# Post-norm attention and FP4 feed-forward block, eight batches on one core: a value projection moved across the batch boundary, and the last batch stripped of its look-ahead

## The reference

```python
x = layernorm(x + attention(x, w_qkv))        # 16 heads of 32, softmax over 1024 keys, scale 1/sqrt(512)
xq, hq = fp4(x), fp4(silu(gate) * y)          # blockwise FP4 (blocks of 16), gate and y are xq @ fp4(w_gate).T, xq @ fp4(w_up).T
x = layernorm(x + hq @ fp4(w_down).T)         # inner width 1408
```

## Time and profile before

| | us |
|---|---|
| median of 3 runs | 3785.34 (3785.06 to 3785.47) |
| the profiled execution's own time | 3785.02 |
| its span, first to last instruction | 3783.2 |
| TensorE (PE) busy | 3609.3 (95%) |
| VectorE (DVE) busy | 3116.5 (82%) |
| GpSimd (POOL) busy | 2473.9 (65%) |
| ScalarE (ACT) busy | 1752.2 (46%) |
| mean granted TensorE clock | 0.991 of full |
| chain that ended last | PE 79%, DVE 10%, POOL 2%, DMA 2% |

### The profile page before, as it was taken

One profiled execution on the slowest core, in us unless ns is written; L12 is line 12 of the kernel. 1 busy time (PEld: TensorE's weight loads), 2 busy tenths in 40 slices (PEclk: granted clock), 3 DMA queues, 4 the chain that ended last, 5 costly groups with the idle time before them and its releaser, 6 DMA issues.

```text
span 3783.2 us, 59181 instructions
## 1 busy us (share of the span) xinstructions
PE 3609.3 (95%) x21563; PEld 1602.5 (42%) x21563; DVE 3116.5 (82%) x4894; ACT 1752.2 (46%) x3090; POOL 2473.9 (65%) x1606
## 2 busy tenths in 40 slices
PE   3799999999999999999999999999999999999999
PEld 2344444344444444343444444434444344434344
DVE  9877898778977889777887789878897778977888
ACT  3466424663256622565236642366424663256622
POOL 2288645985469844797448964588545984479844
PEclk8999999999999999999999999999999999999999
DMA  5211232012311133111331122201232112310133
GB/s 180 88 28 35 67 70 63 25 40 68 73 47 35 35 79 70 47 28 34 89 73 32 35 63 66 71 18 44 64 72 55 30 39 72 75 48 27 32 89 71
DMA packets 358962, 215.21 MB, mean 57 GB/s; under 512 B 280592, under 2 KB 307984, under 8 KB 358544
## 3 DMA queue, kind: packets, MB, share of 16 engines
q1 hardware_dynamic: 358672, 211.43, 21.7%
HBM read 76.28 MB, written 19.66 MB: 25 GB/s over the span
## 4 chain that ended last, share of the span: by engine, by line
PE 79%; DVE 10%; issue 2%; DMA 2%; POOL 2%; ACT 1%; SPq 0%; DVEq 0%; ACTq 0%; POOLq 0%
PE SC L1686 18%; PE CT L1650 10%; PE R L709 9%; PE SC L1635 9%; PE R L689 8%; DVE mx L619 6%; PE R L1686 6%; PE R L1708 6%; PE CT L1708 6%; PE R L699 4%; PE R L721 2%; PE R L731 1%; POOL wd L1236 1%; DVE split L613 1%; DMA split<-split 1%
## 5 line engine op out<-in xcount | busy, mean ns | idle before, releaser
L619 DVE TENSOR_REDUCE mx<-R 128x1 f32<-128x512 f32 x2080 | 1315.8, 683 | 352.7 <-PE R L709 347.8
L1374 ACT ACTIVATE arena<-SC 128x512 f32<-128x512 f32 x1364 | 756.6, 602 | 351.8 <-PE SC L1635 321.7
L1686 PE MATMUL SC<-wgu,split 128*128 128x512 f16 (+1 forms) x3456 | 717.5, 366 | 27.0 <-DMA split<-split 26.9
L1236 POOL TENSOR_TENSOR wd<-wd,arena 128x1024 f32<-128x1024 f32 x224 | 534.7, 2413 | 79.2 <-DVE wd L1495 79.2
L1686 PEld LDWEIGHTS SC<-wgu,split 128*128 128x128 f16 x3456 | 338.9, 99 | 388.5 <-DMA split<-split 37.4
L1266 POOL TENSOR_TENSOR arena<-arena,sc_h 128x512 f32<-128x512 bf16 (+2 forms) x144 | 178.0, 1250 | 465.6 <-DVE arena L542 465.6
L1374 ACT ACTIVATE wd<-SC 128x512 f32<-128x512 f32 x684 | 387.5, 602 | 182.3 <-PE SC L1635 170.0
L689 PE MATMUL R<-xT,wqkv 128*128 128x512 bf16 x1632 | 422.5, 380 | 19.5 <-DVE xT L606 13.1
L709 PE MATMUL R<-ks_even,qs_even 96*128 96x512 bf16 x1056 | 386.2, 383 | 21.5 <-DVE mx L619 11.6
L1411 ACT ACTIVATE arena<-SC,gain 128x512 f32<-128x512 f32 (+1 forms) x192 | 125.0, 651 | 574.1 <-PE R L1686 289.6
L709 PE MATMUL R<-arena 96*128 96x512 bf16 x1024 | 374.0, 382 | 14.6 <-DVE xT L606 6.5
(11 more groups left out here) (152 smaller groups left out, 5309.1 us busy)
## 6 DMA issues: line engine op xcount, KB each, us to landing
x<-n_L_attn_embeddings_dram SPq DMA_DIRECT2D x136, 256.0 KB, 3.1
wd<-wd_kept SPq DMA_DIRECT2D x32, 512.0 KB, 4.4
out_dram<-x SPq DMA_DIRECT2D x64, 256.0 KB, 3.4
ks_even<-split SPq DMA_DIRECT2D x204, 64.0 KB, 2.0
qs_even<-split SPq DMA_DIRECT2D x408, 32.0 KB, 1.9
arena<-split SPq DMA_DIRECT2D x192, 64.0 KB, 2.0
arena<-split SPq DMA_DIRECT2D x384, 32.0 KB, 1.9
wd<-wd_kept SPq DMA_DIRECT2D x16, 384.0 KB, 5.6
```

Of the source, the lines that this page charges most:

```text
L619: nc.vector.reduce_max(mx[:, j:j + 1], ring_of(ring, job)[:, :], AX_X).then_inc(max_done, 1)
L1236: nc.gpsimd.tensor_tensor(acc[u % 2][i], acc[u % 2][i], probs_of(s)[:, hs, :], ALU.add).then_inc(pool_sum, 1)
L1374: nc.scalar.activation(probs_of(s)[:, hd, :], SC[e % SLOTS][:, :], ACT.Exp, scale=SCALE).then_inc(exp_done, 1)
L1686: last = nc.tensor.matmul(GU[kk % 2][which][:, 0:w], xhT[i % 2][:, part_x * KH + k, :], wgu[:, part_w * KH + k, which * I + first:which * ...
```

## The change

Value job 4 leaves u7 in every batch and stands in `first_jobs` ahead of job 5: two of its quarters in front of the last `weigh`s, its other two and the four of job 5 behind `neg`. In the last batch everything meant for a ninth is left out: transpositions of x with their loads, the ten projections, the 32 maxima of u7 with their `neg`, the stacks, `stack_maxima` for the unit behind the last and the saving of x; `first_sums` of the last unit stands at the start of its step 2, since there are no maxima to count. In the last batch's u5 and u6 (units 61 and 62 of 64) GpSimd adds up to tile 6 instead of tile 7, and TensorE's `sum` takes tile 7.

```diff
-        ((4, (1, 2, 3)), (0, 2, 2, 2, 2, 2, 2, 0)), ((4, (4,)), (1, 1, 1, 1, 0, 0, 0, 0)))
+        ((4, (1, 2, 3)), (0, 2, 2, 2, 2, 2, 2, 0)), ((4, ()), (0, 0, 0, 0, 0, 0, 0, 0)))
...
 def pool_sums(u):
-    return POOL_SUMS[u % UNITS]
+    return POOL_SUMS[u % UNITS] - (1 if u in range(UNITS * B - 3, UNITS * B - 1) else 0)
...
+def for_next(kind, a):
+
+    return kind == "xT" or kind.startswith("proj") and a >= GROUPS or kind in ("max", "neg") and a >= UNITS
+
+
 def of_batch(b, places):
 
-    return tuple([(kind, a + b * PER_BATCH.get(kind, GROUPS), j) for kind, a, j in place] for place in places)
+    return tuple([(kind, a + b * PER_BATCH.get(kind, GROUPS), j) for kind, a, j in place
+                  if b < B - 1 or not for_next(kind, a)] for place in places)
...
 def first_jobs(b):
 
-    v = quarters(GROUPS, PROJ_JOBS - 1)
+    v = quarters(GROUPS, PROJ_JOBS - 2) + quarters(GROUPS, PROJ_JOBS - 1)
     return of_batch(b, (v[0:2], [("sum", UNITS - 1, 0), ("neg", UNITS, 0)] + v[2:]
                         + [("sumT", UNITS - 1, 0)], [("ctx", UNITS - 1, 0)]))
...
-                    load_x(x_next, TILES * b)
-                    load_x(x_next, TILES * b + 1)
+                    if b < B - 1:
+                        load_x(x_next, TILES * b)
+                        load_x(x_next, TILES * b + 1)
...
-                        stack_maxima(UNITS * b + u + 1)
+                        if u < UNITS - 1 or b < B - 1:
+                            stack_maxima(UNITS * b + u + 1)
...
                     def keep_x(i):
+                        if b == B - 1:
+                            return
                         sp.wait_ge(x1_done, TILES * b + i + 1)
...
-                    projected(GROUPS * (b + 1), PROJ_JOBS - 1)
+                    for j in (PROJ_JOBS - 2, PROJ_JOBS - 1) if b < B - 1 else ():
+                        projected(GROUPS * (b + 1), j)
                     first_norm(at + 1)
...
                         n_max = 0
+                        if u == UNITS * B - 1 and t == FIRST_SUM_STEP:
+                            first_sums(u)
                         for kind, a, j in jobs:
...
-                    maxima_transposed(last + 1)
+                    if b < B - 1:
+                        maxima_transposed(last + 1)
                     reciprocals(last)
```

More of the change, by code:

```diff
@@ L214, in __init__ @@
                     turn.append(slot)
+            if not ffn:
+                self.last_in.append(dict(last_in))
     def full(self, job):
@@ L1127, in units @@
                         g, used = GROUPS * b + u // 2 + 1, GROUP * TILES * (UNITS * b + u)
-                        turns = [t + 2 for t, (turn_u, _) in enumerate(X_TURNS) if turn_u == u and t + 2 < TILES]
+                        turns = [t + 2 for t, (turn_u, _) in enumerate(X_TURNS) if turn_u == u and t + 2 < TILES and b < B - 1]
                         if u == UNITS - 2:
@@ L1131, in units @@
                                 load_turn(t)
-                        if u >= 2 and u % 2 == 0:
-                            for name in STACKS if u < UNITS - 2 else STACKS[0:2]:
+                        if u >= 2 and u % 2 == 0 and u < UNITS - 2:
+                            for name in STACKS:
                                 stack(g, name, used)
-                        if u == UNITS - 1:
+                        if u == UNITS - 2 and b < B - 1:
+                            for name in STACKS[0:2]:
+                                stack(g, name, used)
+                        if u == UNITS - 1 and b < B - 1:
                             stack(g, STACKS[2])
@@ L1139, in units @@
                                 load_turn(t)
-                        stack_maxima(UNITS * b + u + 1)
+                        if u < UNITS - 1 or b < B - 1:
+                            stack_maxima(UNITS * b + u + 1)
                         if u == UNITS - 3:
-                            load_turn(turns[-1])
+                            for t in turns[-1:]:
+                                load_turn(t)
                 def load_down(b, c):
@@ L1201, in _ @@
                     tiles(b, x_next, out[b, :, :].rearrange("(p t) n -> p t n", t=TILES))
[L1202 to L1204 removed]
+                sp.wait_ge(m_loaded, 32 * (UNITS * B - 1))
+                stacks_done(sp, GROUPS * B - 1)
+                sp.wait_ge(x_kept, 16 * TILES * (B - 1))
                 for par in range(2):
@@ L1446, in tiles @@
                     second_norm(last - 2)
-                    projected(GROUPS * (b + 1) + 1, 0)
+                    if b < B - 1:
+                        projected(GROUPS * (b + 1) + 1, 0)
                     second_norm(last - 1)
-                    projected(GROUPS * (b + 1) + 1, 1)
+                    if b < B - 1:
+                        projected(GROUPS * (b + 1) + 1, 1)
                     second_norm(last)
-                    for j in range(2, QK_JOBS):
+                    for j in range(2, QK_JOBS if b < B - 1 else 0):
                         projected(GROUPS * (b + 1) + 1, j)
@@ L1607, in tiles @@
                     second_moments(i - 1)
-                    projected_low(GROUPS * (b + 1) + 1, 0)
-                    projected_low(GROUPS * (b + 1) + 1, 1)
+                    for j in range(2 if b < B - 1 else 0):
+                        projected_low(GROUPS * (b + 1) + 1, j)
                     add_ffn(i)
                     second_moments(i)
-                    for j in range(2, QK_JOBS):
+                    for j in range(2, QK_JOBS if b < B - 1 else 0):
                         projected_low(GROUPS * (b + 1) + 1, j)
```

3 lines of the change are left out of this document (2 added, 1 removed).

## The result

The changed kernel takes **3758.98 us** (median of 4 runs, 3758.57 to 3760.89) against 3785.4 for the kernel before (4 runs beside it, 3785.06 to 3789.2): a ratio of 0.9929, with a 95% interval of 0.9917 to 0.9942, so 26.4 us less. The prediction was 3757.5, between 3748 and 3765. The profiled execution is the slowest of the four: its own time is 3760.89 and its span 3759.1.

The account below looks back on a forecast made before the run. TensorE, busy 95% of the span, was taken to bound the kernel, with GpSimd deciding in the last batch. 10.5 + 2.1 + 13.7 + 1.5 = 27.8 us off 3785.0, the median 0.3 higher: 3757.5 us, range 3748 to 3765.

Parts of the forecast that it names:

- The filling: Boundaries to feed-forward: value quarters behind `neg` keep TensorE's clock up for the first gate products, 10.5 us over batches 1 to 6.
- rival 2: Boundaries: the value quarters don't keep the clock up, so 10.5 us are lost from the sum; 3768 us, chance 0.08.
- Rival 4: Boundaries: the six quarters run at the lower clock and delay the gate products 3.9 us, seven times; 3797 us, chance 0.03.
- u7's quarters: u7 of batches 0 to 6: taking out value job 4's four quarters gains 0.3 us a batch, 2.1 us for seven.
- The last batch: Last batch's attention stage: GpSimd decides, its last addition comes 12.0 us earlier, plus 1.7 us on SP; together 13.7 us.
- SP's 1.7 us: Last batch's boundary: the x transposition no longer stands behind `stack_maxima` in SP's queue, so its DMA is issued 1.7 us earlier.
- The pause before u6: Last batch, u5 to u6: GpSimd's 4.54 us wait for `first_sums` shrinks to about 3.1 us, gaining 1.4.
- The pause before u7: Last batch, u6 to u7: GpSimd's 3.12 us wait goes since u7 has no maxima, gaining 3.1 us.
- Rival 3: Last batch's units: the clock falls as TensorE stops and starts behind GpSimd, costing half the 13.7 us; 3764 us, chance 0.14.
- The tail: End of the last `down`: without projections everything behind comes 1.3 us earlier; 0 to 1.8 us possible, 1.5 taken.
- Rival 1: Last batch: GpSimd doesn't bind and the batch follows TensorE, gaining 25 instead of 13.7 us; 3746 us, chance 0.10.
- Rival 5: Last batch: the ninth batch's work was all hidden, so only moving value job 4 pays; 3773 us, chance 0.02.

Follow-up runs that it names:

- sp_first: Changed kernel with the first x tile's transposing DMA issued ahead of the next batch's maxima DMAs in batches 0 to 6; 3752.97 us, ratio 0.9914.
- q_late: Kernel before, with value job 4's four quarters in steps 1 to 4 of u7 instead of 0 to 3; 3787.48 us, ratio 1.0001.
- sum_early: Changed kernel with u6's `sum` placed ahead of step 2's maxima and scores in the last batch's u7; 3759.82 us, ratio 0.9928.
- fill_u7: Changed kernel with three spare transpositions behind each of six score products in the first two steps of the last u7; 3758.29 us, ratio 0.9932.
- after_again: The changed kernel itself, unaltered, timed once more on another chip; 3758.74 us, ratio 0.9933.
- warm_last: Changed kernel with spare transpositions on TensorE in the last batch's pause before the gate products; 3760.86 us, ratio 0.9935.
- sp_warm: Changed kernel with the edits of sp_first and warm_last together; 3750.15 us, ratio 0.9912.
- all_three: Changed kernel with the edits of sp_first, warm_last and fill_u7 together; 3751.86 us, ratio 0.9916.
- pool7: Changed kernel with tile 7 given back to GpSimd in both u5 and u6 of the last batch; 3766.99 us, ratio 0.9947.
- pool7_u6: Changed kernel with tile 7 given back to GpSimd in u6 of the last batch alone; 3764.24 us, ratio 0.9937.
- last_only: Changed kernel with value job 4 put back in u7 of batches 0 to 6, leaving only the last batch's changes; 3774.99 us, ratio 0.9967.
- move_only: Kernel before, with only value job 4 moved out of u7, in all eight batches; 3773.38 us, ratio 0.9961.

## Why the prediction was right, and where it was not

The time was 1.5 us from the forecast, but errors of both signs stand behind that, and that they cancel so closely is luck. Read by span, where the terms can be measured, the sum of 27.8 us met 24.1. The median is 1.9 us below the profiled execution, the slowest of the four.

- **The filling (10.5 us): right, 8.8 of it came in the profiled execution.** From the first gate product to the last `down`, batches 0 to 6 lost 8.4 us together. Batches 1, 2, 4, 5 and 6 went from a cold start to 2.76 us; batch 3 kept 4.45, which is the missing 1.7. Five of six cold starts went, so rival 2 is out. Rival 4, a clock that falls in the filling, didn't come: the filling ran at 1.00.
- **The landing: a term that the sum did not have.** I took the data to come at 9.9 us after the last exponential, as before. From there to the gate products it took 9.57, 9.67, 9.58, 11.22, 10.99, 10.23 and 9.93 us, against 9.55, 10.18, 10.66, 9.96, 9.71, 9.96 and 9.84: 1.6 us won in batches 1 and 2, 2.9 lost in 3 to 6, 1.3 lost in all. The sums' transposition ended 9.2 to 9.28 us after the last exponential (the prediction's times give 9.3), so the forecast that it ends just ahead of the data held, and the filling was not what delayed them. The late ones, batches 3 to 6, are those with an instruction packet in flight; before the change these were batches 1, 2, 3 and 5. `sp_first` shows what the step was worth that I had left in SP's queue: some 6 us.
- **u7's quarters (2.1 us): mis-sized, and placed in the wrong unit.** 5.2 us came, 0.7 a batch instead of 0.3, and in u6's length. I had asked only what VectorE and GpSimd could gain in u7, and not what the quarter in step 0 delayed: u7's first scores, for which its first exponentials wait. u7 itself went from 26.6 to 26.54, as forecast. `q_late` adds that reordering alone is worth nothing; the work had to go.
- **The last batch (13.7 us): right in direction, 11.6 measured, and two of its steps failed.** SP's 1.7 us came as forecast (from last exponential to gate product, 9.58 to 7.95). GpSimd's last addition came 10.0 us earlier in the batch (85.48 us after the start of u5 instead of 95.49), not 12.0. The first sums of u5 gave 0.6 (0.7 forecast). The additions taken away gave theirs: 29.60 to 24.98 us of adding in u5 and 30.64 to 24.44 in u6, where the latter also lost its slow first addition. From the first addition of u7 to the last it took 16.51 instead of 17.57 us, mostly because the first was no longer slow there either; the sum had no term for that. The pause before u6, "still about 3.1 us", stayed at 4.52, for the same reason as below: step 2's exponentials behind `sum`. The pause before u7, for which the prediction has 3.1 us gained since "VectorE adds as soon as the exponentials are there", grew by 2.5. The 2.6 us of loss that I had put behind it, at the context, stood here instead: the context's addition waited for nothing. What failed at both pauses is one step: I had GpSimd wait for VectorE's sums, when its first addition needs step 2's exponentials, and these stand behind `sum`, which stands behind GpSimd's own last addition. I had seen that `sum` "holds the exponentials of step 2 back" but let only the context pay. Before u6 that way took 4.52 us at full clock; before u7 the lower clock made it 5.65, as it did in part in all eleven kernels with the stripped last batch. This is read from the waits; the two runs made to shorten it, `sum_early` and `fill_u7`, changed nothing. A smaller slip: the trace shows 12 splits that VectorE loses in u5 to u7 (eight of x, four of projections), not 20; with the 32 reductions it is still more than TensorE loses.
- **Rival 3 came in part.** The clock fell inside u7 at 3543.4 for 3.4 us, right over the serial way (1.1 us), and again at 3563.9, and at the gate products at 3574.1. The window of the first (TensorE busy 2.81 of 3.40 us with 13 products):

```profile
3543.40:3546.80 3.40, 2.81 (x13) 0.70 (x17) 2.16 (x2) 1.03 (x2) 0.00 (x0) 0.50 0.00 0
```

  Where it falls differs between kernels that are the same there: the pause before u6 is 4.52 us in the changed kernel, `after_again`, `sum_early`, `warm_last` and `sp_warm`, whose clock stays up there, and 5.95 to 6.66 in `sp_first`, `fill_u7`, `all_three`, `pool7_u6` and `last_only`, whose clock falls. The Trainium skill (TensorE: Matmul & The Clock Gate, "A second HAM failure mode") says that small idle times between groups of products can make the clock go down and up again; this trace agrees, with 0.89 over u7, where the earlier trace rows had 1.00.
- **The tail (1.5 us): right.** From the first gate product to the last `down` 178.53 became 177.38 (1.15; 1.3 forecast), and from there to the end 7.65 became 7.21 (0.4): 1.6 in all, with the clock up through both pauses.

Together, by span: 8.4 + 5.2 - 1.3 + 11.6 + 1.6 = 25.5, less the 1.3 us that the start was late, is 24.2, against the 24.1 measured. Rival 1 fails by `pool7`, as said above. Rival 5 fails by `last_only`'s 12.2 us.

**What stays open.** The late landings go with the instruction packets, but how one delays the other, and why the packets come earlier from batch to batch, is not shown; issuing the DMA first avoids them in six of seven batches. Nor is it settled what decides, at equal pauses, whether the clock falls (batch 4 of `move_only`, batches 3 and 4 of `after_again` against batch 3 here). Whether `sum_early` would pay at full clock wasn't separable. A version whose `sum` of u6 reads another buffer than the one that step 2 fills was not tried.

## What to carry to other kernels

A pause that hides a transfer isn't free if the engine starts cold behind it: real work moved into it pays twice, once for its old place and once for the clock. Issue the transfer on which the next stage starts ahead of every other one that is ready at that time. When work is taken off an engine in the last pass of a loop, follow each buffer's release to the next engine's first instruction, not only busy times: the gain ends at the longest serial way, and a thinned engine may run slower.

## What was not expected of the hardware

- VectorE's addition of two fp32 tiles in SBUF (128x1024) takes 1.2 us by itself, but 2.1 in the changed kernel and 6.7 in `pool7`, when it is issued while GpSimd adds one pair of tiles after the other: it ends 1.1 us after GpSimd's last one in both (3544.34 after 3543.25, 3552.95 after 3551.86). The Trainium skill (GPSIMD Engine Reference, its table of properties) names contention on the shared SBUF interfaces when VectorE has two SBUF inputs. The trace agrees for GpSimd's addition next to it (3.20 us instead of 2.35), but an addition of VectorE issued into a running series of GpSimd's is the one that waits, and by much more.
- The same transposing DMA landed 2.8 us after its issue where it was on time, and 4.39 and 4.93 us after it in batch 3 of two kernels. Issued ahead of the two small DMAs it came 2.8 us after its issue in batches 0 to 5. In all 94 boundaries where TensorE waited for it, it was late when a 16 KB instruction packet was in flight beside it, and only then.
- A pause of 1.9 us, with the engine busy throughout the 9.2 us ahead of it, was followed by the lower clock in the changed kernel (4.45 us for twelve products), as were seven more of 2.0 to 2.5 us in five other kernels; others of 2.0 to 2.5 us, in `after_again`, `move_only` and `pool7`, were not.
